# A cross-attention and quantised-FFN kernel: x normalised in rows, stored to a scratch in device memory and read back as blocks, by DMAs that ScalarE issues

## What is computed

```
ln(x)  = (x - mean) / sqrt(var + 1e-5)              over the last axis
scores = ln(x) @ ctx^T / 0.72                       per batch, 512 x 512
attn   = softmax(scores) * mask
x1     = x + (attn @ ctx + bias) @ W
h      = ln(x1);  s = max(max|h|, 1e-6) / 127;  h_q = round(h / s)
out    = x1 + (h_q @ Wq^T) * s * w_scale + ffn_bias
```

## Time and profile before

| | us |
|---|---|
| median of 3 runs (lowest, highest) | 338.14 (337.81, 338.71) |
| the profiled execution | 337.69 |
| its span, first to last instruction | 335.9 |
| PE busy | 326.7 (97%) |
| DVE busy | 308.5 (92%) |
| POOL busy | 236.5 (70%) |
| ACT busy | 227.2 (68%) |
| granted clock of PE, mean | 0.999 |

### The profile page before, as it was taken

One profiled execution on the slowest core, in us unless ns is written; L12 is line 12 of the kernel. 1 busy time (PEld: TensorE's weight loads), 2 busy tenths in 40 slices (PEclk: granted clock), 3 DMA queues, 4 the chain that ended last, 5 costly groups with the idle time before them and its releaser, 6 DMA issues.

```text
span 335.9 us, 6071 instructions
## 1 busy us (share of the span) xinstructions
PE 326.7 (97%) x1582; PEld 261.2 (78%) x1582; DVE 308.5 (92%) x630; ACT 227.2 (68%) x455; POOL 236.5 (70%) x368
## 2 busy tenths in 40 slices
PE   8999999999999999999999999999999999999992
PEld 8887777777877778787777878777788877787781
DVE  3988899999899999999999999999999999999887
ACT  5378576768566677766667776667777666777651
POOL 5382677777778777787877778777777878767542
PEclk9999999999999999999999999999999999999999
DMA  7979654645446654454665545456554546400002
GB/s 219 294 196 231 142 128 142 168 132 144 121 135 163 177 149 126 135 148 131 169 172 141 138 138 144 127 169 172 144 129 125 162 129 170 141 33 31 31 33 95
DMA packets 64545, 47.67 MB, mean 142 GB/s; under 512 B 20112, under 2 KB 51088, under 8 KB 64528
## 3 DMA queue, kind: packets, MB, share of 16 engines
q1 hardware_dynamic: 64528, 47.47, 52.3%
HBM read 35.13 MB, written 8.39 MB: 130 GB/s over the span
## 4 chain that ended last, share of the span: by engine, by line
PE 71%; DVE 9%; issue 2%; ACT 1%; DMA 1%; DVEq 0%; SPq 0%
PE ps_attn L517 7%; PE ps_scores L517 7%; PE ps_scores L519 7%; PE ps_attn L519 7%; PE ps_scores L518 7%; PE ps_attn L518 7%; PE ps_ffn L680 7%; PE ps_vw L517 6%; PE ps_vw L518 6%; PE ps_vw L519 6%; PE ps_pt L509 3%; DVE ffn_out L955 1%; DVE abs_max L968 1%; DMA xq_t<-x_int 1%; PE ps_xt L603 1%
## 5 line engine op out<-in xcount | busy, mean ns | idle before, releaser
L756 ACT ACTIVATE x_norm<-x_blocks,norm_spread 128x128 f32<-128x128 f32 x124 | 51.2, 483 | 2.3 <-ACT norm_spread L749 1.5
L1211 POOL TENSOR_TENSOR ct_lo<-ct_raw,ct_hi 128x512 fp32r<-128x512 f32 x28 | 36.4, 1299 | 21.4 <-ACT ct_hi L734 21.4
L517 PE MATMUL ps_attn<-vw_hi,pt_hi 128*128 128x512 f32 x124 | 51.4, 415 | 0.0
L517 PE MATMUL ps_vw<-w_hi,ct_hi 128*128 128x512 f32 x116 | 50.6, 436 | 0.0
L517 PE MATMUL ps_scores<-ct_hi,xt_hi 128*128 128x512 f32 x124 | 48.7, 393 | 0.0
L858 ACT ACTIVATE x_neg<-x,meanvar 128x512 f32<-128x512 f32 x31 | 22.5, 724 | 38.6 <-DVE meanvar L1127 38.6
L519 PE MATMUL ps_scores<-ct_hi,xt_lo 128*128 128x512 f32 x124 | 48.5, 391 | 0.0
L518 PE MATMUL ps_scores<-ct_lo,xt_hi 128*128 128x512 f32 x124 | 48.4, 390 | 0.0
L519 PE MATMUL ps_attn<-vw_hi,pt_lo 128*128 128x512 f32 x124 | 48.4, 390 | 0.0
L518 PE MATMUL ps_attn<-vw_lo,pt_hi 128*128 128x512 f32 x124 | 48.3, 389 | 0.0
L1164 POOL TENSOR_TENSOR scaled<-meanvar,scale 128x2 f32<-128x2 f32 x32 | 16.5, 515 | 44.7 <-DVE meanvar L917 44.7
(11 more groups left out here) (164 smaller groups left out, 776.1 us busy)
## 6 DMA issues: line engine op xcount, KB each, us to landing
x_in<-in_x_dram SPq DMA_DIRECT2D x32, 256.0 KB, 3.1
mask_in<-in_mask_BxSxS_fk_dram SPq DMA_DIRECT2D x32, 256.0 KB, 3.8
out_dram<-out_tile SPq DMA_DIRECT2D x31, 256.0 KB, 2.2
x_blocks<-in_x_dram SPq DMA_DIRECT2D x60, 128.0 KB, 3.5
ctx_in<-in_ctx_dram SPq DMA_DIRECT2D x56, 128.0 KB, 2.7
ctx_in<-in_ctx_dram SPq DMA_DIRECT2D x4, 256.0 KB, 3.7
x_blocks<-in_L_xattn_weights_dram SPq DMA_DIRECT2D x4, 256.0 KB, 6.0
xq_t<-x_int SPq DMA_TRANSPOSE x26, 2.4
```

The lines of the kernel that those rows point to most:

```text
L517: nc.tensor.matmul(bank_, lhs_hi(t), rhs_hi(t), start=(t == 0), stop=False)
L756: last = nc.scalar.activation(x_norm[:, k, a * P:(a + 1) * P], x_blocks[:, slot(n, 4), a * P:(a + 1) * P], ACT.Identity, bias=norm1_spread ...
L1211: nc.gpsimd.tensor_tensor(ct_lo[:, batch_of(n), :, j * P:(j + 1) * P], ct_raw[:, slot(n, 2), :, :], ct_hi[:, batch_of(n), :, j * P:(j + 1) ...
```

## The change

x is no longer read twice. ACT normalises x_in, one row in a partition, with norm1 of the row in one instruction (normalise), and stores x_norm to a new array in device memory, norm_rows (store_rows, one DMA of 256 KB, rows of 2 KB). Later it waits until that store has landed and reads the tile back as blocks with four DMAs of 64 KB into x_blocks (load_rows). DVE's turn_x reads x_blocks. SP's loads of x_blocks, the spreading of norm1 (norm1_masked, same_lane, own_block, spread_norm, norm_spread) and their instructions on POOL, PE, ACT and DVE go.

Where things stand now: in ACT's step, load_rows of tile d+2 follows pt_hi, normalise of tile d+3 follows x_neg, store_rows of tile d+3 follows vw_hi. Ahead of the steps ACT normalises and stores tile 1; step 0 begins with load_rows of tile 1, behind waits for w_lo_ready and bias_terms_ready, since w_raw lies in the memory of x_blocks. In the loop DVE does x_mean_var behind xt_lo, and inv_sum and meanvar2 right behind stats2, ahead of scale_ffn. POOL converts wq ahead of norm_factors of tile 2, SP turns wq in step 0 instead of step 1, and POOL's sum into x_in waits for x_norm of the same tile.

```diff
+    norm_rows = nc.dram_tensor("norm_rows", [TILES * P, D], F32, kind="Internal").ap()
...
+def wait_blocks(eng, sems, base, n):
+    eng.wait_ge(sems[slot(n, 2)], base * (8 * QUADS) + 8 * QUADS * (n + n % 2))
+def wait_rows(eng, sem, base, n):
+    if isinstance(base, int):
+        if base + n > 0:
+            eng.wait_ge(sem, 16 * (base + n))
+    else:
+        eng.wait_ge(sem, base * 16 + 16 * n)
...
 SP
-            sp.wait_ge(w_lo_ready, NT)
-            sp.wait_ge(bias_terms_ready, NT)
-            load_blocks(x_blocks, x_rows, 1 * P, 1, 1, x_blocks_loaded)
-            load_blocks(x_blocks, x_rows, 2 * P, 2, 2, x_blocks_loaded)
...
-                n = d + 3
-                if n % 2 == 0 and exists(base, n):
-                    wait_count(sp, x_norm_ready, base, n - 4 + 2)
-                    load_blocks(x_blocks, x_rows, row + n * P, n, 2, x_blocks_loaded)
...
-                if is_tile(base, d, 1):
+                if is_tile(base, d, 0):
                     sp.wait_ge(wq_rows_ready, 1)
                     for o in range(NT):
                         sp.dma_start_transpose(wq_t[:, :, o * P:(o + 1) * P], wq_rows[:, o, :]) \
...
 PE
-                elif exists(base, d + 2):
-                    spread_norm(d + 2)
...
 ACT
             def normalise(base, n):
-                k = slot(n, 2)
-                wait_count(act, spread_done, base, n)
...
+                k = slot(n, 4)
+                wait_count(act, norm1_ready, base, n + 1)
+                wait_rows(act, norm_rows_stored, base, n - 2)
+                nc.scalar.activation(x_norm[:, slot(n, 2), :], x_in[:, slot(n, 8), :], ACT.Identity,
+                                     bias=norm1[:, k, 1:2], scale=norm1[:, k, 0:1]).then_inc(x_norm_ready, 1)
+            def store_rows(base, n, row):
+                wait_count(act, x_norm_ready, base, n + 1)
+                act.dma_start(norm_rows[bass.ds(row, P), :], x_norm[:, slot(n, 2), :]).then_inc(norm_rows_stored, 16)
+            def load_rows(base, n, row):
+                quads = norm_rows[bass.ds(row, P), :].rearrange("(a i) d -> i a d", i=BLOCK)
+                wait_rows(act, norm_rows_stored, base, n)
+                for b in range(QUADS):
+                    blocks = x_blocks[b * BLOCK:(b + 1) * BLOCK, slot(n, 4), :]
+                    act.dma_start(blocks.rearrange("i (a c) -> i a c", a=QUADS),
+                                 quads[:, :, b * P:(b + 1) * P]).then_inc(x_blocks_loaded[slot(n, 2)], 16)
...
+            normalise(HEAD, PER_BATCH + 1)
+            store_rows(0, 1, 1 * P)
...
+                if is_tile(base, d, 0):
+                    act.wait_ge(w_lo_ready, NT)
+                    act.wait_ge(bias_terms_ready, NT)
+                    load_rows(base, d + 1, (base + d + 1) * P)
...
-                    normalise(base, d + 1)
+                    normalise(base, d + 2)
+                    store_rows(base, d + 2, (base + d + 2) * P)
...
-                if exists(base, d + 2):
-                    normalise(base, d + 2)
                 if exists(base, d):
                     wait_count(act, pt_done, base, d + 1)
                     nc.scalar.activation(flat(pt_hi[:, slot(d, 2), :, :]), ps_pt[:, :],
                                          ACT.Copy).then_inc(pt_hi_ready, 1)
+                if exists(base, d + 2):
+                    load_rows(base, d + 2, (base + d + 2) * P)
...
+                if exists(base, d + 3):
+                    normalise(base, d + 3)
                 if exists(base, d + 4):
                     split_vw(base, d + 4, ps_vw)
+                if exists(base, d + 3):
+                    store_rows(base, d + 3, (base + d + 3) * P)
...
 DVE
             def turn_x(base, n):
-                wait_count(dve, x_norm_ready, base, n + 1)
+                wait_blocks(dve, x_blocks_loaded, base, n)
                 wait_count(dve, xt_lo_ready, base, n - 1)
-                turn_blocks(xt_raw[:, slot(n, 2), :, :], x_norm[:, slot(n, 2), :], xt_raw_ready)
+                turn_blocks(xt_raw[:, slot(n, 2), :, :], x_blocks[:, slot(n, 4), :], xt_raw_ready)
...
-                if exists(base, d):
+                if exists(base, d) and not in_loop(base):
                     nc.vector.reciprocal(col(inv_sum, d), col(prob_sum, d)).then_inc(inv_sum_ready, 1)
-                if in_loop(base):
-                    x_mean_var(d + 3)
...
                 if exists(base, d + 1):
                     split_x(base, d + 1, flat(xt_raw[:, slot(d + 1, 2), :, :]))
+                if in_loop(base):
+                    x_mean_var(d + 3)
...
                     wait_count(dve, stats2_ready, base, n + 1)
+                    if in_loop(base):
+                        nc.vector.reciprocal(col(inv_sum, d), col(prob_sum, d)).then_inc(inv_sum_ready, 1)
+                        nc.vector.bn_aggr(meanvar2[:, slot(n, 4), :],
+                                          stats2[:, slot(n, 4), :]).then_inc(meanvar2_ready, 1)
...
 POOL
-                wait_count(pool, norm1_ready, base, n + 1)
-                wait_count(pool, spread_done, base, n - 2)
-                nc.gpsimd.tensor_tensor(norm1_masked[:, slot(n, 2), :, :],
...
-            for a in range(1 - QUADS, QUADS):
-                nc.gpsimd.affine_select(out=same_lane[:, :], in_=same_lane[:, :], compare_op=ALU.not_equal, fill=1.0,
...
+            norm_factors(HEAD, PER_BATCH + 1)
+            pool.wait_ge(wq_loaded, 16)
+            nc.gpsimd.tensor_copy(flat(wq_rows[:, :, :]), flat(wq_words[:, :, :]).bitcast(I8)) \
+                .then_inc(wq_rows_ready, 1)
+            norm_factors(HEAD, PER_BATCH + 2)
...
-                        pool.wait_ge(x_norm_ready, 1)
+                    wait_count(pool, x_norm_ready, base, d + 1)
```

More of the change, by code:

```diff
@@ L65 @@
 TAIL_STEPS = PER_BATCH + 2
-FILLS = 8
+FILLS = 7
 WARM_UPS = 7
@@ L166, in xattn_ffn_kernel @@
         scale1 = sb("scale1", [P, 2])
-        same_lane = sb("same_lane", [P, P])
-        own_block = sb("own_block", [P, QUADS, 2])
         eps1 = sb("eps1", [P, 1])
@@ L917, in x_mean_var @@
                 nc.vector.bn_aggr(meanvar1[:, slot(n, 4), :], stats1[:, slot(n, 4), :]).then_inc(meanvar1_ready, 1)
-            nc.vector.memset(own_block[:, :, :], 0.0).then_inc(own_block_ready, 1)
-            dve.wait_ge(own_block_ready, 1)
-            for a in range(QUADS):
-                nc.vector.memset(own_block[a * BLOCK:(a + 1) * BLOCK, a, :], 1.0).then_inc(own_block_ready, 1)
             x_statistics(HEAD, PER_BATCH)
```

62 lines of the change are left out of this document (9 added, 53 removed).

## The result

The changed kernel takes **344.26 us** (median of 4 runs, 343.06 to 345.02) beside 338.02 us (337.81 to 338.71) for the kernel before on the same chip: ratio 1.0169, interval 1.0147 to 1.0191, so 1.7% slower. The forecast was 338.7 us, about no change, and its range ended at 343.4: wrong in size and in direction. The profiled execution has a span of 343.2 us, 7.3 more than before; at 345.02 us it is the longest of the four, 0.8 above the median.

What follows compares the result with a forecast made beforehand. PE was taken to bound the loop, with no idle time in a 9.78 us step. Start +3.7, loop -4.8 and tail +1.7 sum to +0.6; on 337.69 plus 0.45 that gave 338.7 us, range 335.9 to 343.4.

Steps and rivals of the forecast that it cites:

- The loop: Loop: without the spread product on PE a step falls from 9.78 to 9.58 us, -4.8 us in 24 steps.
- rival (c): Loop: POOL's rstd is late and DVE waits; step 9.68, loop gains only 2.4, total 341.1 us; chance 0.08.
- rival (b): Loop: ACT becomes the bound, up to 9.8 us a round, so the loop gives nothing; 343.8 us; chance 0.12.
- The 50 ns: ACT's load issues: the skill page's dispatch time, making four loads cost 0.2 us; the prediction noted SP's rows nine times longer.
- The tail: End: loads of tiles 30 and 31 go out too late on ACT, so xt_raw waits; +1.7 us.
- The start: Start: tile 1's store must land before ACT loads it, with ct_hi(4) and exp(0) waiting behind; +3.7 us.
- Rival (a): Start and tail: waits on ACT's in-order queue outweigh the loop; +4.0, 342.1 us; chance 0.20.

Runs made afterwards that it cites:

- e6: Changed kernel with one 8-column product that nothing reads put back on PE in each loop step; 349.74 us, ratio 1.0349 to the kernel before.
- e7: Changed kernel with DVE's x_mean_var back ahead of xt_lo in the loop, behind a small unread reciprocal; 343.14 us, ratio 1.0155 to the kernel before.
- e5: Changed kernel with the loads of tiles 30 and 31 issued by SyncE instead of ScalarE; 342.86 us, ratio 1.0134 to the kernel before.
- e2: Changed kernel with SyncE issuing nothing of step 0 until the store of tile 1 has landed; 341.73 us, ratio 1.0092 to the kernel before.
- e1: Changed kernel with SyncE's four wq transposes issued only after the stores of tiles 1 and 2 landed; 343.61 us, ratio 1.0146 to the kernel before.
- e8: Changed kernel with SyncE loading tiles 1, 2, 30, 31, x_in(4) and mask(2) behind tile 1's loads, transposes behind tile 2's; 337.53 us, ratio 0.9971 to the kernel before.

## Why the prediction was wrong

**The loop (right).** Forecast -4.8, from 9.78 to 9.58 a step; measured -5.1, from 9.84 to 9.63 as means over the 24 steps. e6 shows that it is PE's product. DVE's wait for x_neg went, nothing took its place, scaled fell to 0.20 and for the reason given (e7); rival (c) did not come true, with 0.10 us to spare. Issues do run beside the ACTIVATE ahead of them: the loads go out at 304.46, pt_hi started at 304.45. At 0.45 us each they were as estimated; rival (b) is out for four loads and shown for eight. The 50 ns that the prediction takes from "DMA: Bandwidth & Descriptors" of the Trainium skill stand in a section on DMAs that GpSimd issues, "Anatomy of one DMA"; they do not give the length of ScalarE's issues, and the measured 0.45 decides. Small slips in the prediction's sums (DVE's 9.38 for the row's 9.39, +4.1 where 33.9 less 29.88 is 4.0) are under 0.1 us and change nothing.

**The tail (right).** Forecast +1.7, measured +1.9, with the two waits of xt_raw where they were foretold, and e5 takes them away.

**The start (wrong), at two terms.** The first: "A store of 256 KB lands in 2.2 us [...] I add 1.0, an estimate, for one of them: 3.2". Measured 5.5 (4.6 to 6.4 in the profiles with this start), +2.3. And x_norm(1) itself came 1.3 us later than taken, 17.61 for 16.3; the experiments have it anywhere from 16.2 to 18.1, so that part may be no more than how starts vary. ct_hi(4) came at 25.89 instead of 22.5. e2 shows what the landing consists of: 2.2 us of its own, exactly the row's, and 3.3 of what SyncE has in flight. I had seen these loads move forward and counted only one; there are four in front, and the DMA share at 16 to 24 us, 1.07 and 1.00, is the trace's sign of them. The Trainium skill, "DMA: Bandwidth & Descriptors", section "Issuing engines are not separate DMA queues", says that DMAs of all issuing engines end up on the same 16 engines and interleave; e2 and e1 agree, 5.5 to 2.2 and 6.1 to 2.5.

The second is the larger lesson: the prediction counted the loads of tile 2 as "beside" pt_hi and gave the wait for their store **no term at all**. The store goes out behind x_norm(2) at 29.42, some 3 us ahead of where its loads are wanted, and it met the four transposes and the 1.5 MB of loads queued behind them, which the prediction costed at nothing since "SP mostly waits". That asks what SyncE does, not what its transfers do to others. Which of the two held the store stays open: e1 moved both, and in e2, with the transposes in flight but that 1.5 MB issued behind the store, it took 3.5 us. ScalarE was idle for 4.27 us there. From ct_hi(4) to neg_max(1) it took 14.8 us instead of 11.4. Together +3.4 and +3.4 are the error of 6.8 at neg_max(1). In the profiles with this start (e5, e6 and e7 have it too) the stretch from ct_hi(4) to neg_max(1) takes 13.6 to 14.8 us; in e1, where only the second wait is gone, 12.7. So that wait is 1 to 2 us of the second 3.4. The rest fits PE's lower clock, for which the prediction has no term either ("nothing in the change touches that"); no run separates it. In e8, with neither wait and the clock at 1.00, the stretch is 10.8 us, less than the 11.4 forecast.

Rival (a) named the mechanism, waits on ScalarE's in-order queue, and priced it at 342.1; its bound of +5.5 for the start still had a landing of 3.2 us and no second wait, and the condition that it hung on, issues that do not run beside the ACTIVATE ahead, did not come true. Rival (b) came closest in time, 343.8, by luck: its mechanism did not occur. The prediction's own signs at the start failed as well, exp(0) at 26.43 instead of 22 to 24 and neg_max(1) at 40.73 instead of 33.5.
